# One core, a two-block transformer: in the attention layers, the value products of a chunk's two key tiles are put one behind the other

## The reference

```python
# latent (layer 0)
attn = jnp.einsum('bhnd,bhsd->bhns', q, k) * scale          # k rotated before
attn = jax.nn.softmax(jnp.clip(attn, -11.0, 11.0), axis=-1)
out = jnp.einsum('bhns,bhsd->bhnd', attn, v)
...
# cross (layer 1)
scores = jnp.einsum('bshk,bthk->bhts', k, q)
probs = jax.nn.softmax(scores, axis=-1)
attn = jnp.einsum('bhts,bshk->bthk', probs, v)
...
# self (layer 1)
scores = jnp.einsum('bhid,bhjd->bhij', q * scale, k)
attn = jnp.einsum('bhij,bhjd->bihd', jax.nn.softmax(scores, axis=-1), v)
```

## Time and profile before

| | |
|---|---|
| median of 3 runs | 3606.59 us (3606.55 to 3608.03) |
| profiled execution, first to last instruction | 3601.8 us |
| mean granted TensorE clock, share of 2.4 GHz | 0.882 |
| PE busy | 2645.3 us, 73% |
| DVE busy | 2401.7 us, 67% |
| POOL busy | 1429.5 us, 40% |
| ACT busy | 1384.5 us, 38% |

### The profile page before, as it was taken

One profiled execution on the slowest core, in us unless ns is written; L12 is line 12 of the kernel. 1 busy time (PEld: TensorE's weight loads), 2 busy tenths in 40 slices (PEclk: granted clock), 3 DMA queues, 4 the chain that ended last, 5 costly groups with the idle time before them and its releaser, 6 DMA issues. The chain is left out here.

```text
span 3601.8 us, 38810 instructions
## 1 busy us (share of the span) xinstructions
PE 2645.3 (73%) x11472; PEld 1632.8 (45%) x11472; DVE 2401.7 (67%) x3617; ACT 1384.5 (38%) x1913; POOL 1429.5 (40%) x1019
## 2 busy tenths in 40 slices
PE   3987987997996867887788778777877354646465
PEld 3555554554553754544454445444544222323232
DVE  4886786787785764666466646664665586877775
ACT  2553552552552004544354425543553231313121
POOL 3663662563562012343334324432443253443434
PEclk9998998998998877999999889998999676767676
DMA  2010010010101120000000000000000100000000
GB/s 57 14 31 22 14 31 17 15 35 1 30 9 36 47 59 14 13 5 27 22 14 5 27 21 14 5 27 21 14 5 0 38 12 5 25 0 29 0 18 6
DMA packets 109968, 70.48 MB, mean 20 GB/s; under 512 B 15011, under 2 KB 109795, under 8 KB 109795
## 3 DMA queue, kind: packets, MB, share of 16 engines
q1 hardware_dynamic: 109796, 68.44, 6.4%
HBM read 60.03 MB, written 8.39 MB: 19 GB/s over the span
## 5 line engine op out<-in xcount | busy, mean ns | idle before, releaser
L726 ACT ACTIVATE cross_probs<-cross_scores 128x1024 f32<-128x1024 f32 x256 | 259.3, 1024 | 379.8 <-PE cross_scores L938 376.8
L852 DVE TENSOR_REDUCE cross_part<-cross_ring 128x1 f32<-128x512 f32 x512 | 333.0, 686 | 78.4 <-PE cross_ring L1013 75.2
L726 ACT ACTIVATE latent_probs<-latent_scores 128x1024 f32<-128x1024 f32 x256 | 259.1, 1025 | 226.1 <-PE latent_scores L938 202.9
L1013 PE MATMUL cross_ring<-cross_S,cross_Q 128*128 128x512 f32 x512 | 219.3, 475 | 152.9 <-DVE cross_part L852 77.5
L938 PE MATMUL latent_scores<-latent_Q,latent_S 128*128 128x512 f32 x1024 | 295.1, 422 | 28.2 <-issue 17.8
L938 PE MATMUL cross_scores<-cross_Q,cross_S 128*128 128x512 f32 x1024 | 297.7, 420 | 6.0 <-ACT cross_probs L726 2.6
L1046 PE MATMUL latent_outT<-latent_probs,latent_VN 128*64 128x512 f32 x1024 | 264.6, 625 | 15.5 <-DVE latent_probs L873 15.3
L1046 PE MATMUL cross_outT<-cross_probs,cross_VN 128*64 128x512 f32 x1024 | 270.4, 629 | 0.0
L482 POOL TENSOR_TENSOR cross_acc<-cross_probs 128x1024 f32<-128x1024 f32 x32 | 79.8, 2493 | 437.7 <-ACT cross_probs L726 437.7
L482 POOL TENSOR_TENSOR latent_acc<-latent_acc,latent_probs 128x1024 f32<-128x1024 f32 x64 | 153.7, 2402 | 229.0 <-DVE latent_probs L873 229.0
L938 PEld LDWEIGHTS latent_scores<-latent_Q,latent_S 128*128 128x128 f32 x1024 | 191.3, 199 | 111.9 <-issue 53.4
(11 more groups left out here) (300 smaller groups left out, 6531.7 us busy)
## 6 DMA issues: line engine op xcount, KB each, us to landing
latent_WRAW<-in_L_xattn_Wkv_dram SPq DMA_DIRECT2D x64, 128.0 KB, 2.3
latent_C<-in_ctx_dram SPq DMA_DIRECT2D x4, 1024.0 KB, 6.4
latent_WRAW<-in_L_xattn_Wq_dram SPq DMA_DIRECT2D x32, 128.0 KB, 2.3
cross_C<-in_ctx_dram SPq DMA_DIRECT2D x4, 1024.0 KB, 8.6
cross_WRAW<-in_L_xattn_Wq_dram SPq DMA_DIRECT2D x32, 128.0 KB, 2.3
cross_WRAW<-in_L_xattn_Wk_dram SPq DMA_DIRECT2D x32, 128.0 KB, 2.4
cross_WRAW<-in_L_xattn_Wv_dram SPq DMA_DIRECT2D x32, 128.0 KB, 2.3
latent_XN<-in_x_dram SPq DMA_DIRECT2D x4, 512.0 KB, 3.9
```

Source lines behind the costliest of these rows:

```text
L726: nc.scalar.activation(probs[h][c % 2][:, :, :], scores[h][:, :, :], ACT.Exp).then_inc(exp_done, 1)
L852: nc.vector.reduce_max(part[:, h, qt, i:i + 1], bank[:, :], AX.X).then_inc(taken, 1)
L1013: nc.tensor.matmul(bank[:, :], Q1[nxt][:, h, qt * P:(qt + 1) * P], S1[nxt][:, h, i * 512:(i + 1) * 512], start=True, stop=True).then_inc(f ...
```

## The change

`attend_order` put the two value products of a chunk's tiles into two slots with filling units between them. Now both stand in the first slot, ahead of the softmax item, and the second slot is empty. The units that stood between them and those that stood behind the second now all stand behind both. The numbers in `BEHIND` are as before.

```diff
--- before.py
+++ after.py
@@ -122,7 +122,7 @@
     for c in range(NC):
         order += [[("S", 0, c)], [("S", 1, c), ("soft", 0, c)]]
         if c or late:
-            order += [[("AV", c - 1, 0), ("soft", 1, c)], [("AV", c - 1, 1)]]
+            order += [[("AV", c - 1, 0), ("AV", c - 1, 1), ("soft", 1, c)], []]
         else:
             order[-1] += [("soft", 1, c)]
     order[-1] += [("end",)]
```

## The result

The changed kernel takes 3660.99 us (median; 3658.37 to 3662.31), the kernel before, on the same chip, 3607.31: a ratio of 1.015, 95% interval 1.0136 to 1.0163, or 54 us slower. The forecast was 3596.1 with a range up to 3612. The profiled span of after is 3660.2 us at a mean granted clock of 0.865 (before: 3601.8 at 0.882).

A forecast was written before the change was run, and what follows sets the result against it. PE was taken to bound cross, PE and DVE nearly latent, DVE self. Terms -24.2 + 7.2 + 0 - 3.6 + 7.5 + 0 + 2.6 = -10.5 us took the median from 3606.6 to 3596.1; range 3583 to 3612.

The forecast's parts named there:

- place B: Cross, chunk 3, steps 1 to 6: second value pair moves into idle time ahead of `shift` of head 1; 24.2 us gained.
- place A: Cross, chunk 1, 24 places: value pair moves ahead of the first `max`; zero by order, 7.2 us lost by clock.
- (a): Cross step 6, three times: statistics ahead of the first row maximum make the third `max` later; 1.5 us lost each.
- cross, change of batch: Cross, steps 6 and 7 at the three changes of batch: 2.5 us lost each, 7.5 us in all.
- (b): Cross step 7, chunk 1: pair ahead of `kv` 3 and `kT` 0 makes keys and first `max` 0.9 us later.
- (c): Other chunks of cross step 7: give and take 0.1 to 0.4 us of row maxima; together +0.1.
- latent, end of batches: Latent, end of batches 1 to 3: second pair goes into `kT` 0's wait for GpSimd; 1.2 us each, 3.6 gained.
- latent, other steps: Latent loop: one `kv` unit comes behind the pair, while turned keys wait for GpSimd anyway; 0.
- self, other steps: Self loop steps: pair moves ahead of `shift` into idle time, but PE then waits for DVE; 0.
- self, entering step: Self step entering a batch, three times: pair ahead of last gate, `k` and `q`, chain 0.9 us later; 2.6 lost.
- the slower rival: Cross: clock falls at every place A, slowing both score blocks; 43 us lost there, 3633 in all; chance 0.11.
- The cover just holds: Cross, after place B: `folded` ready at 1514.19, head 1 of `sum` needs it at 1514.4; without cover 0.2 us lost.

## Why the prediction was wrong

Its terms against what each part measured alone (a ratio's distance from 1 times 3607 us):

| term | forecast, us | measured, us (95%) |
|---|---|---|
| place B, 24 steps | -24.2 | -20 (-26 to -13) |
| place A, 24 steps, with (a), the statistics of step 6 | +7.2 + 4.5 | +58 (+52 to +64) |
| cross, change of batch, step 7: (b) and (c) | +3.0 | +15.5 (+10 to +21) |
| latent, end of batches | -3.6 | -7 (-11 to -4) |
| latent, other steps | 0 | +5 (+1 to +8) |
| self, other steps | 0 | -1 (-5 to +2) |
| self, entering step | +2.6 | not measured alone; its three steps are 4 us longer in the trace of after than in that of the other steps' run |
| sum | -10.5 | +50, and the last; whole change: +54 |

That the sum comes so near the whole is partly luck: the larger terms are known to 5 or 6 us each.

**Place A is the step that failed**, and in it the sentence "I take half of the 24 places at 0.6 us". The order was read rightly: idle times of 0.67 and 2.53 us, the third `max` 3.26 us behind the first, as before. Both factors after that were too small. *How often:* 18 of 24 places in the changed kernel, 22 of 24 with A alone, instead of 12. I split evenly, since the earlier trace rows held one outcome of each kind; but both rows were of other places, with other work ahead, and the "emptier" PE that the slower rival points to was the better comparison. *How much:* 1.8 to 3.0 us in the loop and not 0.6. Together that is 48 us over steps 1 to 6 (980.0 us in after, 932.0 with place B alone, the 5.6 of step 6 from above included), not 7.2. I let the `max` products, paced by DVE at 0.66 us each, hide the slow stretch. They don't: in the slow stretch DVE gets through two row maxima in 1539.69 - 1538.11 = 1.58 us and not in 1.3, because the two products take PE 1.39 us and each engine waits for the other in turn (DVE 0.88, then twice 0.29 us, against 0.47 once where the clock held). Over the kernel this is in the 50 us on the line of the row maxima. The second block of scores, 3.7 us behind the first, was cited against the rival, and lies in the slow stretch with it. The upper bound of 21.6 had the same fault (one block, 0.9 us), so the range, up to 3612, could not hold the 3661.

The slower rival named this mechanism and its price nearly: 24 x 1.8 = 43 us and 3633 in all. It fell short by 27 (27 against 54 us): 21.5 at place A and cross's change of batch (43 + 9 against 58 + 15.5), 4 of B's gain, 5 in latent's steps, less 3.6 of latent's ends. A chance of 0.11 for it was the misjudgement. The place to read it was the trace's own warning: twice 1.52 us of waiting with 1.7 us of products between them, and the clock at 1.00; the change takes more than half of what is between. The Trainium skill's page "TensorE: Matmul & The Clock Gate", section "A second HAM failure mode: psum-queue depth-cycling", describes a kernel whose brief but frequent idle times between groups make the clock swing, with the time lost in warming up again. The trace agrees with it here (2.53 us idle, 1.8 to 3.0 us lost), and I had set it aside on the strength of one row. That by it all 24 places would pay was my reading and not the page's, which names no length of idle time; 18 did.

**Place B was right**, in mechanism and nearly in size: idle time ahead of `shift` 0.70 us (forecast 0.6), 20 of 24 us. The step alternates between 37.6 and 38.5 to 38.9 us in the loop, mean 38.0, where 37.8 was forecast. "The cover just holds" failed: `folded` comes 0.4 us after the start of `sum`, where I had it just in time, and takes 0.3 us of each 1.01 back.

**The change of batch in cross** was right in sign. Its 7.5 us were for two steps. (a), in step 6, was read rightly: 1.95 us of statistics, the third `max` 2.2 us later, 5.9 us in the three steps with the clock's part, forecast 4.5. (b), the keys' chain, fits: the first `max` waits 1.1 us more (0.9 forecast), +2 us (-1 to +5) against 2.7. What failed is (c), "together +0.1": step 7 as a whole costs 15.5 us against the 3.0 of (b) and (c), most of it (11.4 us more of PE busy) by a lower clock, to which I gave no price here.

**Latent:** the idle time at the ends was worth 2.4 us a batch by the medians (1.3 to 3.6) instead of 1.2; the 1.7 that I had read as the most to be had lies within that. The sixth step's loss was missing. I had priced this very effect for cross (statistics ahead of the first row maximum), and for latent only named it, in the section on the change (ahead of a clip of head 1), and left it out of the sum.

**Self** was right for the loop.

## What to carry to other kernels

Before moving work out of a gap, add up the idle time on both sides of what is moved: if two waits of the tensor engine become one, price the fall of its clock at every repetition and over all that follows the wait (here 1.8 to 3.0 us a time, at 18 of 24 places), and make that the forecast unless a row of the same place shows otherwise. A general rule for an order ("always together") should be tried place by place: here one place was worth -20 us and another +58. Where work is placed by a count of items, each edit of the list moves it, so look again at who stands behind it.

## What was not expected of the hardware

- Two waits of 1.52 us with 1.7 us of products between them left the clock at 1.00 in cross's loop; 0.67 and 2.53 us brought it down in most steps, and so did 0.67 and 1.84 us with 1.43 of work between, which is less waiting in all. The same idle times gave both outcomes in neighbouring steps, so the length of the wait alone doesn't decide.
- The clock stays at 0.51 for 6.8 us although PE is busy for 6.25 of them; in the loop of after such a stretch lasts 6.8 or 10.2 us, with place A alone also 3.4.
- Eight copies of a 128x512 product (2.58 us for ten) in the wait keep the clock up in the loop and cost nothing; three copies (1.43 us for five) don't keep it up in 21 of 24 steps.
- The end of a loop's body costs PE 0.51 us behind a product whose work is done, against none where the loop is written out; it was worth nothing here, as PE waits again later.
